# Softmax normalisation of an attention stage: the sums' reciprocal over 128 partitions, by way of DRAM

## The chip, the cores and the metric

One Trainium2 chip, all 8 cores. Each core computes one of the 8 batch rows, with no exchange between cores. The metric is the device time of the slowest core in microseconds.

## The reference

A layer on x of 8 x 2048 x 1024: layer norm, then attention (16 heads of 64, causal, with a linear position bias) and a gated FFN with quantised activations and ternary weights, both added to x. The part that is touched is the softmax division:

```
xn = layernorm(x)
scores = einsum('bhqd,bhkd->bhqk', q, k) / sqrt(64) + alibi_bias   # -inf above the diagonal
attn = softmax(scores, axis=-1)
out = einsum('bhqk,bhkd->bhqd', attn, v)
x = x + out @ w_out + b_out + ffn(xn)
```

## The kernel before

The program is written as one list of instructions; each engine takes its own in that order, and waits are counted semaphores. `B.op` makes every instruction of an engine other than TensorE wait for the one before it on its engine. `B.dma` issues on a named queue: "sync" is SP's, "gpsimd" is POOL's; a `gate` is waited for on that queue first, so everything behind it on the queue waits too.

Phases: layer norm with V projection, attention (from about 440 to 1390 us in the trace), output projection, FFN gate and up, FFN down. Beside the first two phases a generator (`pump`) quantises the three FFN weight matrices: a pass with an Abs on ScalarE (L693) for each of 32 tiles, then a pass with three VectorE operations (L723, L725, L728) and a store by POOL. The tiles are loaded by SP into two buffers.

Attention runs over 8 head pairs (hp). Each begins with the Q and K projection (L446, L450; evicted by ScalarE, L460 and L464). Then come two blocks qh of two 512-column query groups j each. A block walks over key steps (j, ki), ki being a tile of 128 keys. A step issues for both heads (loc 0, 1): the score matmul (L568), the exponential on ScalarE (L581), and on the diagonal memsets and a triangular mask on VectorE (L591, L595). The PV matmul (L501) of step si - 2 follows. V has a column of ones, so row 64 of the output bank is the softmax sum. Score banks rotate over three for each head, `SPOOL`; a bank is free when its reader has finished. Every second step pumps once.

When the last key of a group is done, `_norm_part1` copies the sum row (ScalarE, L522) into `srow`, the 64 output rows into `o_un` (L524), and starts a reciprocal on one partition (VectorE, L527). `part2` broadcasts the reciprocal to 64 partitions by an fp32 matmul with a row of ones (L536) into the first score bank of its head, multiplies (VectorE, L542), and stores to `s_attn` (POOL). `part2` is put into `norm_pending`; a step runs one of them when more than three are pending, in the last block (hp 7, qh 1) when any is. Norms are numbered 0 to 63 in the prediction, in this order; even ones are loc 0, odd ones loc 1.

Of the kernel before, what the change touches and what calls it, by code (L numbers as in the profile page):

```python
# [11 lines left out]
F32 = mybir.dt.float32  # L12
BF16 = mybir.dt.bfloat16
AF = mybir.ActivationFunctionType
ALU = mybir.AluOpType
# [84 lines left out]
class Builder:  # L100
    def __init__(self):
        nc = bass.Bass("TRN2", target_bir_lowering=False)
        self.nc = nc
        self.sched = []
        self.C = defaultdict(int)
        self.stack = contextlib.ExitStack()
        self.sem = {s: self.stack.enter_context(nc.semaphore(s))
                    for s in ("TS", "VS", "SS", "GS", "SY")}

        d = nc.dram_tensor  # L110
        self.x = d("x", [L, D], F32, kind="ExternalInput").ap()
        self.w_in = d("w_in", [D, 3 * D], F32, kind="ExternalInput").ap()
        self.b_in = d("b_in", [3 * D], F32, kind="ExternalInput").ap()
        self.w_out = d("w_out", [D, D], F32, kind="ExternalInput").ap()
        self.b_out = d("b_out", [D], F32, kind="ExternalInput").ap()
        self.w_gate = d("w_gate", [INNER, D], F32, kind="ExternalInput").ap()
        self.w_up = d("w_up", [INNER, D], F32, kind="ExternalInput").ap()
        self.w_down = d("w_down", [D, INNER], F32, kind="ExternalInput").ap()
        self.y = d("y", [L, D], F32, kind="ExternalOutput").ap()
        self.s_xnb = d("s_xnb", [L, D], BF16).ap()  # L120
        self.s_n = d("s_n", [L, D], BF16).ap()
        self.s_attn = d("s_attn", [D, L], BF16).ap()
        self.s_acc = d("s_acc", [L, D], F32).ap()
        self.s_mg = d("s_mg", [INNER, D], BF16).ap()
        self.s_mu = d("s_mu", [INNER, D], BF16).ap()
        self.s_md = d("s_md", [D, INNER], BF16).ap()
        self.s_n2 = d("s_n2", [L, INNER], BF16).ap()

        eb_np, m01_np = _make_consts()
        self.c_eb = nc.inline_tensor(eb_np, name="c_eb")  # L130
        self.c_m01 = nc.inline_tensor(m01_np, name="c_m01")
        self.n_eb = eb_np.shape[1]

        self.fa = Arena(nc, "fa", F32, 8832)
        self.ba = Arena(nc, "ba", BF16, 88320)
# [24 lines left out]
        self.P = [nc.alloc_psum_tensor(f"pb{i}", [128, 512], F32) for i in range(8)]  # L160
        self.bguard = {i: [] for i in range(8)}
# [211 lines left out]
    def ph_attention(self):  # L373
        B = self
        ba, fa = B.ba, B.fa
# [10 lines left out]
        o_un = [ba.alloc(512, parts=65) for _ in range(8)]  # L386
        srow = fa.alloc(2048, parts=1)
        oun_guard = [[] for _ in range(8)]
        B.r_row = fa.alloc(2048, parts=1)
        rr_guard = [[] for _ in range(4)]  # L390
        wstage2 = B.att_wstage
        stg_cons = B.att_stg_cons
        tv = [("TX%d" % p, B.C["TX%d" % p]) for p in range(2)]
# [9 lines left out]
        sa_guard = [[], []]  # L403
        norm_pending = []
        oun_next = [0]

        def emit_norm(maxn=1):
            for _ in range(maxn):
                if not norm_pending:
                    return  # L410
                norm_pending.pop(0)()

        def load_wqk(hp2):
            par2 = hp2 % 2
# [14 lines left out]
        B.waitg("scalar", B.ln_final)  # L429
        B.waitg("vector", B.ln_final)  # L430
        B.ln_final = None
        wq_cast_next = load_wqk(0)
        qk_guard2 = [[], []]
        for hp in range(8):
# [5 lines left out]
            for qk in range(2):  # L440
                for tc in range(4):
# [3 lines left out]
                    for c in range(ND - 1):  # L445
# [3 lines left out]
                            start=(cc == 0), stop=False))  # L449
# [26 lines left out]
            for qh in range(2):  # L476
# [30 lines left out]
                            _norm_part1(loc2, j2, hp, qh, [g])  # L507

                def _norm_part1(loc2, j2, hp2, qh2, vlast):
                    while len(norm_pending) > 3:  # L510
                        emit_norm(1)
                    h2 = 2 * hp2 + loc2
                    jj = j2 % 2
                    obank = OBANK[loc2]
                    Ob = B.P[obank]
                    pu = oun_next[0]
                    oun_next[0] = (pu + 1) % 8
                    B.waitg("scalar", vlast)
                    B.waitg("scalar", oun_guard[pu])
                    ru = pu % 4  # L520
                    B.waitg("scalar", rr_guard[ru])
                    gs0 = B.op("scalar", lambda e, b=Ob, r2=ru: e.copy(  # L522
                        out=srow[0:1, 512 * r2:512 * r2 + 512], in_=b[64:65, :]))
                    gs_ = B.op("scalar", lambda e, b=Ob, p2=pu: e.copy(out=o_un[p2][0:64, :], in_=b[0:64, :]))  # L524
                    B.bguard[obank] = [gs_]
                    B.waitg("vector", [gs0])
                    gr = B.op("vector", lambda e, r2=ru: e.reciprocal(  # L527
                        out=B.r_row[0:1, 512 * r2:512 * r2 + 512],
                        in_=srow[0:1, 512 * r2:512 * r2 + 512]))

                    def part2(loc3=loc2, h3=h2, jj3=jj, qh3=qh2, pu3=pu, ru3=ru, gr3=gr, gs3=gs_):
                        rbank = SPOOL[loc3][0]
                        Rb = B.P[rbank]
                        B.waitg("tensor", [gr3])
                        B.waitg("tensor", B.bguard[rbank])
                        gt = B.op("tensor", lambda e, b=Rb, r2=ru3: e.matmul(  # L536
                            b[0:64, :], B.ones_row64[0:1, :],
                            B.r_row[0:1, 512 * r2:512 * r2 + 512], start=True, stop=True))
                        rr_guard[ru3] = [gt]
                        B.waitg("vector", [gt, gs3])  # L540
                        B.waitg("vector", sa_guard[jj3])
                        gv = B.op("vector", lambda e, b=Rb, p2=pu3, j2=jj3: e.tensor_tensor(  # L542
                            out=o_attn[0:64, 512 * j2:512 * j2 + 512],
                            in0=o_un[p2][0:64, :], in1=b[0:64, :], op=ALU.mult))
                        oun_guard[pu3] = [gv]
                        B.bguard[rbank] = [gv]
                        B.waitg("gpsimd", [gv])
                        sa_guard[jj3] = [B.dma("gpsimd",
                            B.s_attn[64 * h3:64 * h3 + 64, 1024 * qh3 + 512 * jj3:1024 * qh3 + 512 * jj3 + 512],
                            o_attn[0:64, 512 * jj3:512 * jj3 + 512], "SA%d" % jj3)]  # L550
                        B.store_done[h3] = B.store_done[h3] + sa_guard[jj3]
                    norm_pending.append(part2)

                final_blk = (hp == 7 and qh == 1)
                for si, (j, ki) in enumerate(keys):
                    sp = si % 3
                    if len(norm_pending) > (0 if final_blk else 3):
                        emit_norm(1)
                    for loc in locs:
                        st_ = stepmap[loc].get((j, ki))  # L560
                        if st_ is None:
# [46 lines left out]
            wqk_guard[par] = list(qk_guard[-1:])  # L608
            qk_guard2[par] = list(qk_guard[-1:])
            qk_guard = []  # L610
        emit_norm(100)
        B.pump(10 ** 6)
        ba.reset(); fa.reset()
        B.ba.reset()
# [360 lines left out]
```

How the kernel before makes its waits and increments, by code:

```python
    def wait(self, engine, sem, val):  # L171
        if val > 0:
            self.em(engine, lambda e, s=self._sem(sem), v=val: e.wait_ge(s, v))
# [8 lines left out]
    def dma(self, queue, out, in_, sem, transpose=False, slow=False, gate=()):  # L182
        sh = self._sem(sem)
        self.waitg(queue, gate)
        self.C[sem] += 16
        v = self.C[sem]
        if transpose:
            self.em(queue, lambda e, o=out, i=in_, s=sh: e.dma_start_transpose(out=o, in_=i).then_inc(s, 16))
        else:
            self.em(queue, lambda e, o=out, i=in_, s=sh, sl=slow: e.dma_start(out=o, in_=i, allow_slow_non_contiguous=sl).then_inc(s, 16))
        return (sem, v)
# [7 lines left out]
        def run(e, f=fn, sh=self.sem[s], p=prev, vv=v):  # L199
            if p > 0:
                e.wait_ge(sh, p)
            return f(e).then_inc(sh, 1)
```

## Time and profile before

| | us |
|---|---|
| time before, median of 2 runs | 2307.33 |
| the two runs | 2310.09, 2304.57 |
| the profiled execution | 2303.03 |
| its span on the slowest core | 2301.5 |
| spans of the 8 cores | 2279.4 to 2301.5 |

The profile shows one execution on the slowest core, number 6. Times in its rows count from the first instruction. "Idle before" is the time that an engine sat idle ahead of an instruction, and the name behind the arrow is what released it.

### The profile page before, as it was taken

Reading aid. Unit: us, or ns where it says so; the run is one execution under the profiler, and the core shown is the slowest. Engines: PE = TensorE matmul, PEld = TensorE weight load, DVE = VectorE, ACT = ScalarE, POOL = GpSimd, SP = SyncE. Lnnn points to the kernel's source line nnn. Section 1 sums busy time; section 2 is a strip of 40 time slices with the busy share of each in tenths; the row PEclk is TensorE's granted clock in tenths of the full one; section 3 lists DMA queues with packets and bytes.
Section 4 is the critical chain, followed back from the end, with each engine's and each line's share of the span. In section 5 each row is a group of like instructions: output and inputs, shape, how many; then the busy total and the mean of one; then the engine's idle time right before and its main releaser. Section 6 shows DMA issues by size and latency. Waiting matters only on the chain.

```text
span 2301.5 us, 22849 instructions; the slowest of 8 cores (2279.4 to 2301.5 us)
## 1 busy us (share of the span) xinstructions
PE 1429.1 (62%) x5215; PEld 512.3 (22%) x5304; DVE 1009.3 (44%) x1639; ACT 755.7 (33%) x1150; POOL 163.9 (7%) x276
## 2 busy tenths in 40 slices
PE   0004444466756465665647660777999999709997
PEld 0001111111211121111112110223444444304443
DVE  3006667464466764335665430213555555501110
ACT  0762222456644446866445460010122222100000
POOL 2000111100001110000110000000000000000000
PEclk9996666755656565666667575898999999959999
DMA  5774554332334443424543008783000000394661
GB/s 147 245 230 134 182 170 164 122 111 82 112 98 127 146 142 106 140 78 125 161 133 91 18 4 168 230 204 87 37 37 37 37 37 39 75 224 122 153 156 55
DMA packets 277094, 274.27 MB, mean 119 GB/s; under 512 B 208226, under 2 KB 224738, under 8 KB 276964
## 3 DMA queue, kind: packets, MB, share of 16 engines
q1 hardware_dynamic: 256740, 205.68, 33.6%
q0 software_dynamic: 20224, 67.12, 7.7%
q8 instruction: 49, 0.80, 0.1%
q14 instruction: 81, 0.66, 0.1%
HBM read 155.32 MB, written 67.11 MB: 97 GB/s over the span
## 4 chain that ended last, share of the span: by engine, by line
PE 45%; DVE 22%; DMA 12%; ACT 10%; issue 8%; SPq 2%; DVEq 1%; POOL 0%; ACTq 0%; POOLq 0%
PE pb L904 9%; PE pb L824 8%; PE pb L802 8%; DVE fa L527 7%; ACT ba L581 6%; PE pb L446 5%; PE pb L501 4%; PE pb L653 3%; DVE ba L763 3%; PE pb L568 2%; DVE ba L725 2%; DVE ba L723 2%; DMA fa<-w_gate 2%; SPq L188 2%; DMA ba<-s_md 2%
## 5 line engine op out<-in xcount | busy, mean ns | idle before, releaser
L581 ACT ACTIVATE ba<-pb,fa 128x512 bf16<-128x512 f32 (+2 forms) x522 | 339.0, 649 | 266.1 <-PE pb L568 222.2
L501 PE MATMUL pb<-ba 128*65 128x512 bf16 x502 | 230.3, 552 | 184.2 <-DVE ba L595 131.7
L752 PE MATMUL pb<-ba 128*128 128x512 bf16 x251 | 91.8, 528 | 296.3 <-DVE ba L358 169.6
L904 PE MATMUL pb<-ba 128*128 128x512 bf16 x971 | 220.5, 382 | 67.9 <-DMA ba<-s_n 66.9
L527 DVE RECIPROCAL fa<-fa 1x512 f32<-1x512 f32 x64 | 213.8, 3341 | 50.0 <-ACT fa L522 44.7
L568 PE MATMUL pb<-ba 64*128 64x512 bf16 (+2 forms) x502 | 136.7, 516 | 157.5 <-DVE ba L542 156.4
L824 PE MATMUL pb<-ba 128*128 128x512 bf16 x876 | 214.0, 382 | 24.4 <-DMA ba<-s_mu 23.6
L802 PE MATMUL pb<-ba 128*128 128x512 bf16 x875 | 213.1, 381 | 6.6 <-DVE fa L788 5.8
L812 ACT ACTIVATE fa<-pb,fa 128x512 f32<-128x512 f32 x128 | 88.0, 687 | 364.3 <-PE pb L806 364.2
L834 DVE SCALAR_TENSOR_TENSOR fa<-pb,fa 128x512 f32<-128x512 f32 x128 | 96.1, 751 | 157.5 <-PE pb L828 157.2
L904 PEld LDWEIGHTS pb<-ba 128*128 128x128 bf16 x992 | 97.6, 99 | 186.3 <-issue 71.2
L446 PE MATMUL pb<-ba 128*128 128x512 bf16 x433 | 120.6, 421 | 17.6 <-POOL ba L423 14.7
L915 DVE SCALAR_TENSOR_TENSOR fa<-pb,fa 128x512 f32<-128x512 f32 x32 | 24.0, 751 | 244.8 <-PE pb L908 134.9
L536 PE MATMUL pb<-fa 1*64 1x512 f32 x128 | 113.9, 1019 | 21.9 <-DVE fa L527 11.3
L595 DVE TENSOR_TENSOR ba<-ba 128x128 bf16<-128x128 bf16 x256 | 57.7, 226 | 143.3 <-ACT ba L581 94.0
L824 PEld LDWEIGHTS pb<-ba 128*128 128x128 bf16 x896 | 88.2, 98 | 131.3 <-issue 27.1
L802 PEld LDWEIGHTS pb<-ba 128*128 128x128 bf16 x896 | 88.0, 98 | 112.6 <-issue 8.0
L693 ACT ACTIVATE ba<-fa 128x1024 bf16<-128x1024 f32 x96 | 101.5, 1057 | 27.8 <-DMA fa<-w_gate 17.0
L501 PEld LDWEIGHTS pb<-ba 128*65 128x65 bf16 x502 | 44.4, 134 | 296.3 <-issue 296.3
L591 DVE MEMSET ba<- 128x128 bf16 (+2 forms) x247 | 60.6, 245 | 109.1 <-ACT ba L581 45.3
L568 PEld LDWEIGHTS pb<-ba 64*128 64x128 bf16 x502 | 31.8, 98 | 338.8 <-issue 336.2
L752 PEld LDWEIGHTS pb<-ba 128*128 128x128 bf16 x256 | 29.1, 123 | 347.9 <-issue 340.2
(101 smaller groups left out, 1320.5 us busy)
## 6 DMA issues: line engine op xcount, KB each, us to landing
fa<-w_gate SPq DMA_DIRECT2D x64, 512.0 KB, 5.0
fa<-w_up SPq DMA_DIRECT2D x64, 512.0 KB, 3.9
fa<-w_down SPq DMA_DIRECT2D x64, 512.0 KB, 4.1
fa<-x SPq DMA_DIRECT2D x48, 512.0 KB, 5.4
s_n<-ba POOLq DMA_DIRECT2D x32, 512.0 KB, 2.9
fa<-w_in SPq DMA_DIRECT2D x24, 512.0 KB, 6.3
s_mg<-ba POOLq DMA_DIRECT2D x32, 256.0 KB, 5.6
s_mu<-ba POOLq DMA_DIRECT2D x32, 256.0 KB, 4.4
```

What stands on the lines that cost most here:

```text
L446: B.em("tensor", lambda e, b=Pb, cc=c, q=qk, t=tc, p=par: e.matmul(b[:], wqk[p][:, 1024 * q + 128 * cc:1024 * q + 128 * cc + 128], xn_fm[c ...
L501: g = B.op("tensor", lambda e, ob=B.P[obank], k=ki2, hh=h2, pb=pbuf2, f1=first, l1=lastk: e.matmul(ob[0:65, :], v_sb[:, 1040 * k + 65 * hh ...
L527: gr = B.op("vector", lambda e, r2=ru: e.reciprocal(out=B.r_row[0:1, 512 * r2:512 * r2 + 512], in_=srow[0:1, 512 * r2:512 * r2 + 512]))
L536: gt = B.op("tensor", lambda e, b=Rb, r2=ru3: e.matmul(b[0:64, :], B.ones_row64[0:1, :], B.r_row[0:1, 512 * r2:512 * r2 + 512], start=True ...
L568: tg = B.op("tensor", lambda e, b=Sb, l=loc, k=ki, a=wlo, z=whi, kf=k_fm, qf=q_fm: e.matmul(b[0:128, 0:z - a], kf[64 * l:64 * l + 64, 128 ...
L581: eg.append(B.op("scalar", lambda e, b=Sb, q=qg0, g0=gw, a=wlo, c=col, pb=pbuf, jj=j: e.activation(out=pb[:, q - 512 * jj:q - 512 * jj + g ...
L693: gv = B.op("scalar", lambda e, i=idx, c0=col: e.activation(out=sg[0], in_=wb[i], func=AF.Abs, accum_out=accs[:, c0:c0 + 1]))
L752: B.em("tensor", lambda e, b=Pb, cc=c, t=ts_, hh=half: e.matmul(b[:], xn_fm[cc][:, 128 * t:128 * t + 128], wv_sb[:, 1024 * cc + 512 * hh:1 ...
L802: B.em("tensor", lambda e, b=bg_, cc=c, tt=t, o=oc: e.matmul(b[:], n_fm[cc][:, 128 * tt:128 * tt + 128], mg[cc][:, 512 * o:512 * o + 512], ...
L824: B.em("tensor", lambda e, b=bu_, cc=c, tt=t, o=oc: e.matmul(b[:], n_fm[cc][:, 128 * tt:128 * tt + 128], mu[cc][:, 512 * o:512 * o + 512], ...
L834: gh = B.op("vector", lambda e, b=bu_, tt=t, o=oc, hs=h_sb: e.scalar_tensor_tensor(out=hs[:, 512 * o:512 * o + 512], in0=b[:], scalar=B.dq ...
L904: B.em("tensor", lambda e, b=Pb, cc=c, lt=tl, hh=half, nf=n2f: e.matmul(b[:], nf[cc][:, 128 * lt:128 * lt + 128], md[cc][:, 512 * hh:512 * ...
```

## The change

A norm's reciprocal is computed on 128 partitions. POOL writes the sum row to a DRAM scratch `s_d1` and reads it back as 128 x 4. VectorE takes the reciprocal of 128 x 4, splits it into a bf16 high part and a bf16 rest (`rhls`, 128 x 8), with memsets of a scrap tile `vjk` between the steps. SP writes the 128 x 8 to `s_d2` and reads it back as two rows of 512. A matmul with K = 2 and bf16 ones adds the two rows and broadcasts them. The norm is emitted in three deferred pieces with due steps counted from its end (6, 8 and 10), at most two pieces a step; the last block emits all that is pending at every step. More than nine pending pieces force an emission ahead of the next norm.

```
+        self.s_d1 = d("s_d1", [4, 512], F32).ap()
+        self.s_d2 = d("s_d2", [4, 1024], BF16).ap()
...
-        def emit_norm(maxn=1):
-            for _ in range(maxn):
-                if not norm_pending:
+        def emit_norm(maxn=10 ** 6, due=None):
+            n = 0
+            while norm_pending and n < maxn:
+                if due is not None and norm_pending[0][0] > due:
                     return
-                norm_pending.pop(0)()
+                norm_pending.pop(0)[1]()
+                n += 1
...
-                    while len(norm_pending) > 3:
+                    while len(norm_pending) > 9:
                         emit_norm(1)
...
-                    B.waitg("vector", [gs0])
-                    gr = B.op("vector", lambda e, r2=ru: e.reciprocal(
-                        out=B.r_row[0:1, 512 * r2:512 * r2 + 512],
-                        in_=srow[0:1, 512 * r2:512 * r2 + 512]))
+                    B.waitg("gpsimd", [gs0])
+                    d1a = B.dma("gpsimd", B.s_d1[ru], srow[0:1, 512 * ru:512 * ru + 512],
+                                "NB%d" % (ru % 2), gate=g_d1[ru] + last_nb[ru % 2])
+                    g_srow[ru] = [d1a]
+                    d1b = B.dma("gpsimd", s4s[ru], B.s_d1[ru].rearrange("(p c) -> p c", c=4),
+                                "NB%d" % (ru % 2), gate=[d1a] + g_s4[ru])
...
+                    def part2a(ru3=ru, d1g=[d1b]):
+                        B.waitg("vector", d1g)
+                        B.waitg("vector", g_rhlw[ru3])
+                        B.op("vector", lambda e, r3=ru3: e.reciprocal(out=r4b[:], in_=s4s[r3]))
+                        B.op("vector", lambda e: e.memset(vjk[:], 0.0))
+                        B.op("vector", lambda e, r3=ru3: e.tensor_copy(out=rhls[r3][:, 0:4], in_=r4b[:]))
+                        B.op("vector", lambda e: e.memset(vjk[:], 0.0))
+                        B.op("vector", lambda e: e.tensor_copy(out=hif[:], in_=r4b[:]))
+                        B.op("vector", lambda e, r3=ru3: e.tensor_copy(out=hif[:], in_=rhls[r3][:, 0:4]))
+                        B.op("vector", lambda e: e.memset(vjk[:], 0.0))
+                        B.op("vector", lambda e, r3=ru3: e.tensor_tensor(
+                            out=rhls[r3][:, 4:8], in0=r4b[:], in1=hif[:], op=ALU.subtract))
+                        B.op("vector", lambda e: e.memset(vjk[:], 0.0))
+                        gva = B.op("vector", lambda e: e.memset(vjk[:], 0.0))
...
+                    def part2b(ru3=ru):
+                        d2a = B.dma("sync", B.s_d2[ru3].rearrange("(p c) -> p c", c=8), rhls[ru3],
+                                    "NQ%d" % (ru3 % 2), gate=[ev["gva"]] + g_d2[ru3] + last_nq[ru3 % 2])
+                        g_rhlw[ru3] = [d2a]
+                        d2b = B.dma("sync", r2s[ru3].rearrange("t (p c) -> t p c", c=4),
+                                    B.s_d2[ru3].rearrange("(p t2 c) -> t2 p c", t2=2, c=4),
+                                    "NQ%d" % (ru3 % 2), gate=[d2a] + g_r2[ru3])
...
+                    def part2c(loc3=loc2, h3=h2, jj3=jj, qh3=qh2, pu3=pu, ru3=ru, gs3=gs_):
...
-                        B.waitg("tensor", [gr3])
+                        B.waitg("tensor", [ev["d2b"]])
                         B.waitg("tensor", B.bguard[rbank])
-                        gt = B.op("tensor", lambda e, b=Rb, r2=ru3: e.matmul(
-                            b[0:64, :], B.ones_row64[0:1, :],
-                            B.r_row[0:1, 512 * r2:512 * r2 + 512], start=True, stop=True))
-                        rr_guard[ru3] = [gt]
+                        gt = B.op("tensor", lambda e, b=Rb, r3=ru3: e.matmul(
+                            b[0:64, :], ones2[:], r2s[r3], start=True, stop=True))
+                        g_r2[ru3] = [gt]
...
-                    norm_pending.append(part2)
+                    norm_pending.append((st0 + 6, part2a))
+                    norm_pending.append((st0 + 8, part2b))
+                    norm_pending.append((st0 + 10, part2c))
...
-                    if len(norm_pending) > (0 if final_blk else 3):
-                        emit_norm(1)
+                    B.gstep += 1
+                    if final_blk:
+                        emit_norm(10 ** 6)
+                    else:
+                        emit_norm(2, due=B.gstep)
```

## Rows read from the trace of the kernel before

**Rows 1.** Sum over eight stretches of attention, and the page's clock in 40 slices.
```profile
sum 927.00, PE 560.88 PEld 142.86 DVE 503.32 ACT 511.26 POOL 82.52; mean PE 70.11 PEld 17.86 DVE 62.91 ACT 63.91 POOL 10.32
...
PEclk9996666755656565666667575898999999959999
```

**Rows 2.** Waits in attention: who waited for whom, us, times, longest.
```profile
ACT ba L581 <- PE pb L568: 221.1, 60, 12.6
...
ACT fa L522 <- PE pb L536: 18.0, 21, 1.0
...
PE pb L568 <- DVE ba L542: 156.4, 33, 11.4
```

**Rows 3.** Timeline of one pair's end: start, us, engine, line, operation, idle before.
```profile
1302.47 3.67 PE L536 MATMUL pb<-fa 1*64 1x512 f32 x4
...
1303.12 3.34 DVE L527 RECIPROCAL fa<-fa 1x512 f32<-1x512 f32 x1 [1.76 <-ACT fa L522]
...
1310.79 0.68 DVE L542 TENSOR_TENSOR ba<-ba,pb 64x512 bf16<-64x512 bf16 x1
...
1311.62 0.80 PE L568 MATMUL pb<-ba 64*128 64x512 bf16 x2 [5.48 <-DVE ba L542]
...
1312.41 1.47 ACT L581 ACTIVATE ba<-pb,fa 128x512 bf16<-128x512 f32 x2 [6.58 <-PE pb L568]
```

**Rows 4.** The page's groups: reciprocal and fp32 broadcast, busy us, mean ns, idle.
```profile
L527 DVE RECIPROCAL fa<-fa 1x512 f32<-1x512 f32 x64 | 213.8, 3341 | 50.0 <-ACT fa L522 44.7
...
L536 PE MATMUL pb<-fa 1*64 1x512 f32 x128 | 113.9, 1019 | 21.9 <-DVE fa L527 11.3
```

**Rows 5.** Timeline: steady stretches of ScalarE, and a pair of bf16 matmuls.
```profile
915.90 3.03 ACT L581 ACTIVATE ba<-pb,fa 128x512 bf16<-128x512 f32 x4
...
920.27 3.03 ACT L581 ACTIVATE ba<-pb,fa 128x512 bf16<-128x512 f32 x4
...
1325.32 15.52 ACT L581 ACTIVATE ba<-pb,fa 128x512 bf16<-128x512 f32 x20 [0.85 <-PE pb L568]
...
1301.51 1.03 PE L501 MATMUL pb<-ba 128*65 128x512 bf16 x2 [1.26 <-DVE ba L595]
```

**Rows 6.** Small VectorE operations: two of the timeline, one group of the lines.
```profile
6.93 0.06 DVE L236 MEMSET fa<- 128x1 f32 x1 [6.93 <-DMA fa<-b_out]
7.12 0.06 DVE L237 MEMSET fa<- 128x1 f32 x1
...
L351 DVE TENSOR_SCALAR fa<-fa 128x1 f32<-128x1 f32 x16 | 2.5, 154 | 1.7
```

**Rows 7.** DMA issues: two of the timeline, two of the page (KB each, us to landing).
```profile
1.93 2.96 SPq L190 DMA_DIRECT2D fa<-b_in  x3
4.95 0.23 SPq L190 DMA_DIRECT2D fa<-b_out  x1
...
fa<-w_down SPq DMA_DIRECT2D x64, 512.0 KB, 4.1
...
s_attn<-ba POOLq DMA_DIRECT2D x64, 64.0 KB, 2.0
```

**Rows 8.** ScalarE's timeline: three waits of other kinds.
```profile
669.13 10.05 ACT L581 ACTIVATE ba<-pb,fa 128x512 bf16<-128x512 f32 x13 [10.17 <-PE pb L568]
...
868.78 1.47 ACT L581 ACTIVATE ba<-pb,fa 128x512 bf16<-128x512 f32 x2 [2.13 <-PE pb L568]
...
1271.37 9.27 ACT L581 ACTIVATE ba<-pb,fa 128x512 bf16<-128x512 f32 x12 [3.32 <-PE pb L568]
```

**Rows 9.** The last block: timeline of ScalarE, and the chain's last store.
```profile
1340.92 0.58 ACT L522 COPY fa<-pb 1x512 f32<-1x512 f32 x1
...
1354.98 18.63 ACT L581 ACTIVATE ba<-pb,fa 128x512 bf16<-128x512 f32 x24 [0.85 <-PE pb L568]
...
1375.85 0.58 ACT L522 COPY fa<-pb 1x512 f32<-1x512 f32 x1 [2.23 <-PE pb L501]
...
1388.18 2.70 DMA s_attn<-ba
```

More of the change, by code:

```diff
@@ L388, in ph_attention @@
         oun_guard = [[] for _ in range(8)]
-        B.r_row = fa.alloc(2048, parts=1)
-        rr_guard = [[] for _ in range(4)]
+        s4_all = fa.alloc(16)
+        s4s = [s4_all[:, 4 * k:4 * k + 4] for k in range(4)]
+        r4b = fa.alloc(4)
+        hif = fa.alloc(4)
+        vjk = fa.alloc(4)
+        rhl_all = ba.alloc(32)
+        rhls = [rhl_all[:, 8 * k:8 * k + 8] for k in range(4)]
+        r2blk = fa.alloc(1024, parts=2).bitcast(BF16)
+        r2s = [r2blk[0:2, 512 * k:512 * k + 512] for k in range(4)]
+        ones2 = fa.alloc(32, parts=2).bitcast(BF16)
+        g_srow = [[] for _ in range(4)]
+        g_s4 = [[] for _ in range(4)]
+        g_rhlw = [[] for _ in range(4)]
+        g_d1 = [[] for _ in range(4)]
+        g_d2 = [[] for _ in range(4)]
+        g_r2 = [[] for _ in range(4)]
+        last_nb = {0: [], 1: []}
+        last_nq = {0: [], 1: []}
         wstage2 = B.att_wstage
@@ L405, in ph_attention @@
         oun_next = [0]
-        def emit_norm(maxn=1):
-            for _ in range(maxn):
-                if not norm_pending:
+        B.gstep = 0
+        def emit_norm(maxn=10 ** 6, due=None):
+            n = 0
+            while norm_pending and n < maxn:
+                if due is not None and norm_pending[0][0] > due:
                     return
-                norm_pending.pop(0)()
+                norm_pending.pop(0)[1]()
+                n += 1
         def load_wqk(hp2):
@@ L431, in ph_attention @@
         B.ln_final = None
+        g12 = B.op("vector", lambda e: e.memset(ones2[:], 1.0))
+        B.op("vector", lambda e: e.memset(vjk[:], 0.0))
+        B.waitg("tensor", [g12])
         wq_cast_next = load_wqk(0)
@@ L520, in _norm_part1 @@
                     ru = pu % 4
-                    B.waitg("scalar", rr_guard[ru])
+                    B.waitg("scalar", g_srow[ru])
                     gs0 = B.op("scalar", lambda e, b=Ob, r2=ru: e.copy(
@@ new lines, in _norm_part1 @@
+                    g_srow[ru] = [d1a]
+                    d1b = B.dma("gpsimd", s4s[ru], B.s_d1[ru].rearrange("(p c) -> p c", c=4),
+                                "NB%d" % (ru % 2), gate=[d1a] + g_s4[ru])
+                    g_d1[ru] = [d1b]
+                    last_nb[ru % 2] = [d1b]
+                    st0 = B.gstep
+                    ev = {}
+                    def part2a(ru3=ru, d1g=[d1b]):
[10 more added lines that the diff above has]
+                            out=rhls[r3][:, 4:8], in0=r4b[:], in1=hif[:], op=ALU.subtract))
+                        B.op("vector", lambda e: e.memset(vjk[:], 0.0))
+                        gva = B.op("vector", lambda e: e.memset(vjk[:], 0.0))
+                        g_s4[ru3] = [gva]
+                        ev["gva"] = gva
@@ new lines, in part2b @@
+                    def part2b(ru3=ru):
[5 more added lines that the diff above has]
+                                    "NQ%d" % (ru3 % 2), gate=[d2a] + g_r2[ru3])
+                        g_d2[ru3] = [d2b]
+                        last_nq[ru3 % 2] = [d2b]
+                        ev["d2b"] = d2b
@@ L610, in ph_attention @@
             qk_guard = []
-        emit_norm(100)
+        emit_norm(10 ** 6)
         B.pump(10 ** 6)
```

1 line of the change is left out of this document (removed).

## Prediction

> **What bounds the kernel now.** I read the stretches by engine first. The change lies inside attention, from 463 to 1390 us. There no engine is full: in these 927 us TensorE is busy 561, ScalarE 511 and VectorE 503, and the granted clock stands at 5 to 7 tenths, so it is mostly at the lower level, 1.2 GHz [rows 1]. What counts is therefore who waits, and the waits say it: the score exponentials (L581) wait 221.1 us for score matmuls, and these in turn wait 156.4 us for the normalising multiply L542 [rows 2].
>
> One such wait, read from the timeline, shows the reader the pattern [rows 3]. Two heads end a block together. VectorE runs reciprocal, multiply, reciprocal, multiply, and only then (1311.62) may the next score matmul write its bank, since each multiply reads a broadcast that sits in a score bank. ScalarE idles 6.58 us before 1312.41. The reciprocal on one partition costs 3.34 us, 213.8 us over 64 norms; the broadcast as fp32 costs 113.9 us of TensorE, 1.78 a norm [rows 4]. There are 32 such pairs of norms. At the end of a head pair one broadcast falls behind the Q/K projection and costs little, so about three of the four pairs of each head pair give the full wait.
>
> Between the waits ScalarE is the pace: four exponentials (two key steps) start every 4.37 us where a weight tile's Abs (L693) runs on ScalarE, and 1.55 us a step where it doesn't, 20 in 15.52 [rows 5].
>
> **The change, part by part.**
> Removed: 64 long reciprocals and 64 fp32 broadcasts. The new broadcast has K = 2 in bf16; a pair of 512-column bf16 matmuls takes 1.03 us at the low clock [rows 5], so I take 0.5 instead of 1.78. At the end of each head pair a broadcast stands right ahead of the projection, which TensorE alone sets; 7 times about 1.4 us saved there, -10.
>
> Added on VectorE: ten dependent small operations per norm. Five memsets at a pitch of 0.20 us, and five others at 154 ns plus 0.1 us between (1.7 us idle for 16) give 1.0 + 1.3 = 2.3 us [rows 6]. VectorE is thus relieved by only 3.34 + 0.1 - 2.3 = 1.1 us a norm.
>
> Added on POOL's queue: write 2 KB, read it back as 128 x 4. POOL is held until the write has landed, about 2.0 us as the 64 KB store of s_attn [rows 7], plus 0.5 of issue, so some 6 us for two norms. Behind it wait the weight stores and the s_attn stores; weight buffers are two deep, which is 4 steps, 6.2 to 8.7 us. I count this as hidden. The data are wanted 6 key steps later, so the first round trip (about 5 us) is hidden too, outside the last block.
>
> Added on SP's queue: write 128 x 8 bf16, wait, read back as 2 x 128 runs of 8 bytes. The write: 2.1 us as the s_attn store [rows 7]. For the read no row has this shape. Below, b_out, one row on one partition: issued 4.95, VectorE released 6.93, 2.0 us. Above, the b_in loads, two of the three made of 4-byte runs: issued from 1.93, all landed before 6.93, 5.0 us [rows 6, 7]. I take the middle, 3.5 us, since 256 runs lie between one and two thousand. Behind SP wait the weight loads, which land 4.1 us after issue [rows 7] and are issued about 4 steps ahead: nearly hidden, I add 8 us over the stage.
>
> By the Trainium skill, "DMA: Bandwidth & Descriptors", section "Why a DMA increments its semaphore by 16 and not by 1", a transfer is spread over the largest number of engines up to 16 that divides the slowest dimension of both sides. That dimension is 2 for the read back, so two engines would carry 128 runs each; no row here shows such a transfer, and by this rule the upper half of the bracket is the likelier.
>
> **Where the new wait falls.** I counted the emission from the plans. Every norm queues three pieces: (a) the small operations, due 6 steps on, (b) the SP transfers, due 8, (c) broadcast and multiply, due 10. The queue is first in, first out, and two norms enter at the same step. So the first goes at +6, +8, +10, but the second's (a) goes only at +10, behind the first's (c), and its (b) and (c) go together at +11. TensorE meets the wait for a transfer that SP has just been given. This holds for the odd norms 1 to 55, that is 28 times (seven of them through the forced emission above nine pending). Nothing else can run on TensorE, since its queue is in order.
>
> Length of it, from the start of the first broadcast: matmul 0.5, multiply 0.7 and hand-overs 0.2, small operations 2.3, write 2.1, read 3.5, hand-overs 0.3: 9.6 us. The next score matmul ends 1.1 us later, 10.7. TensorE got there 1.1 us after an exponential ended, so ScalarE sees 11.8 us against stored work of three steps: 4.5 us without Abs, about 6.4 with it. It idles 7.3 or 5.4, mean near 6.4. 28 x 6.4 = 179. In the first three head pairs norms come every 3 to 7 steps and the first broadcast waits as well, 12 x 1 = 12. Together 191 us.
>
> What it replaces: 221.1 us of waits of L581, less 22.4 after 1290.8 (last block, below), and 18.0 of L522 for the fp32 broadcasts [rows 2]: 216.7. Not all goes: seven starts of a head pair keep some 1.3 of 3.3 us, the weight pass that ends at 669 and its like keep 12, and short waits of 2.1 us on masks, six of them, 13 [rows 8]. So 216.7 - 9 - 12 - 13 = 183. Net of the regular part: 191 - 183 - 10 + 8 = +6 us.
>
> **The last block** (hp 7, qh 1) empties the list at once. At its first step eleven pieces go out, (b) of norm 56 to (c) of norm 59. First round trip done at 1302.5 + 5.6 + 0.5 + 0.7 = about 1309.6, then three cycles of 9.6: 1338.4, ahead of any score matmul. Before, scores resume at 1311.62 [rows 3], but four old broadcasts slow the next steps until 1325.32 [rows 5]; after, four steps from 1338.4 + 0.9 end at 1345.6. +20. In the middle pair both chains stand in front of the next step, with POOL's trip now uncovered: sums 1341.6 + 4.4 + 2.3 + 5.6 + 1.3 = 1355.2, + 9.6 = 1364.8, two steps to 1368; before 1354.98 [rows 9]. +13. At the end, from 1376.4 the same [rows 9]: 4.4 + 2.3 + 5.6 + 1.3 + 9.6 + store 3.2 = 1402.8, before 1388.18 + 2.70 = 1390.9. +12. Together +45.
>
> **Sum.** 6 + 45 = +51 on the profiled execution of 2303.0 us: 2354. The median shown is 4.3 us above it, so I forecast 2358, +2.2%. Nothing outside attention changes.
>
> **Rivals.** (1) The transfer back is quick, 2.1 us: each of 28 waits is 1.4 shorter, -39, the last block's eight cycles -11: 2308, no change. For it: 2.0 us landings of small transfers; against: 8-byte runs. Chance 0.27. (2) The read takes 5 us, or both transfers queue behind a 512 KB load in SP's ring, 1.5 to 3 more each time: 36 x 1.5 to 3 = +54 to +108: 2412 to 2466. For it: SP's loads are in flight much of the time; against: while SP is held for the second norm it issues none. Chance 0.25. The rule above, with two engines at the price of the upper row, gives the first of these, 2412. (3) Faster: TensorE's wait is covered, for instance because ScalarE holds more stored work or because the old waits freed were larger than I took. Its place is the step +11, its price 6.4 us each; it decides from 28 x 6.4 down to 28 x 2.9, so that the last block's 45 is paid and 46 gained: the chain would have to be 9.6 - 3.5 = 6.1 us or less, of which the parts on TensorE and VectorE and the hand-overs take 4.0 and leave 2.1 for two transfers of 2.0 each. Then about 2250. Chance 0.10. That the reciprocals don't leave the chain is excluded by the code. The forecast itself, 2335 to 2390: 0.38.
>
> **Numbers.** Range 2300 to 2440: it leaves out faster (0.10) and the far end of rival 2 (0.10). A change under 2% can't be told from none here, that is 2261 to 2353. Faster 0.10, within 0.40 (rival 1 and the lower third of the forecast), slower 0.50.
>
> **What would show it.** Right: VectorE's reciprocals gone and its attention share down by about 70 us; the new broadcast with idle of 5 to 8 us before them, released by a transfer into the two-row tile, some 30 times; attention longer by about 50 us, most of it after the start of the last block. Wrong: landings of the SP pair far from 2.1 and 3.5 us; weight loads or stores that reach ScalarE or VectorE late; TensorE's clock falling or rising in attention, which I take as unchanged.

## The result and the profile after

The changed kernel takes 2507.4 us (median of 11 runs) where the kernel before takes 2308.3 (10 runs): ratio 1.0845, 95% interval 1.0819 to 1.0871, so 8.5% slower. The forecast was 2358, at most 2440. Below, a time in us worked out from a ratio is the ratio times 2308; the changed kernel is then 2503. Some runs of either kernel fall into a slower state of the chip, and the ratios leave them out.

All of it lies in attention. The first matmul of the output projection, same core (0), before and after (the lists of one line: duration min/median/max, first to last start):

```profile
L653 PE MATMUL pb<-ba x250: 378/379/634, 1440.6 to 1511.0; 128*128 128x512 bf16 x125
```

```profile
L715 PE MATMUL pb<-ba x250: 378/379/631, 1653.5 to 1723.2; 128*128 128x512 bf16 x125
```

It starts 213 us later; the first projection matmul of attention starts at 416 and 421. Attention with the transposes behind it is thus 208 us longer on this core, and 201 and 196 on cores 2 and 6, against 195 by the ratio.

Waits of the changed kernel (who waited for whom: us, times, longest). L594 is the new broadcast, L599 its multiply, L630 the score matmul, L643 the exponential, L785 and L755 the weight quantisation on VectorE and ScalarE, `s_d` either DRAM scratch:

```profile
ACT ba L643 <- PE pb L630: 371.4, 86, 27.9
...
PE pb L594 <- DMA fa<-s_d: 320.9, 48, 14.0
...
PE pb L630 <- DVE ba L599: 95.7, 28, 10.1
...
DVE ba L785 <- DMA fa<-w_down: 47.2, 12, 8.7
...
ACT ba L755 <- DMA fa<-w_up: 37.8, 10, 7.2
```

The wait that the change was to remove did go down, score matmuls behind the multiply from 156.4 [rows 2] to 95.7 us. But TensorE now waits 320.9 us for the read back from DRAM, and ScalarE 371.4 instead of 221.1. The groups of the reciprocal and the broadcast, which answer to [rows 4]:

```profile
L564 DVE RECIPROCAL fa<-fa 128x4 f32<-128x4 f32 x64 | 11.4, 178 | 37.8 <-DMA fa<-s_d 31.3 <-DVE ba L599 0.5 <-DVE ba L657 0.2
...
L594 PE MATMUL pb<-fa 2*64 2x512 bf16 x64 | 37.5, 586 | 328.8 <-DMA fa<-s_d 320.9 <-ACT ba L643 3.6 <-ACT ba L548 2.4
```

Both did what they should: 213.8 us of reciprocals became 11.4, 113.9 of broadcasts 37.5.

A pair of norms as the forecast described it, in the timeline (start, us, engine, line, operation, idle before):

```profile
1055.61 0.63 PE L594 MATMUL pb<-fa 2*64 2x512 bf16 x1
...
1056.56 0.68 DVE L599 TENSOR_TENSOR ba<-ba,pb 64x512 bf16<-64x512 bf16 x1 [7.58 <-PE pb L594]
...
1057.34 0.18 DVE L564 RECIPROCAL fa<-fa 128x4 f32<-128x4 f32 x1
...
1059.73 0.33 SPq L192 DMA_DIRECT2D s_d<-ba  x1
...
1061.63 0.26 SPq L192 DMA_DIRECT2D fa<-s_d  x1
...
1064.86 0.60 PE L594 MATMUL pb<-fa 2*64 2x512 bf16 x1 [7.08 <-DMA fa<-s_d]
...
1066.20 0.69 ACT L643 ACTIVATE ba<-pb,fa 128x512 bf16<-128x512 f32 x1 [4.08 <-PE pb L630]
```

First broadcast, multiply, small operations, write, read back, second broadcast: 9.25 us where 9.6 were forecast.

Other pairs are worse, and this the forecast did not have. The chain of waits between 1193 and 1224:

```profile
1193.82 4.69 DMA fa<-s_d
...
1201.12 4.32 DMA s_d<-ba
...
1205.92 6.06 DMA fa<-w_down
...
1212.21 0.77 DVE ba L785
...
1214.73 0.69 DVE ba L599
...
1217.89 2.87 DMA s_d<-ba
...
1220.88 2.59 DMA fa<-s_d
...
1223.74 0.61 PE pb L594
```

The first row is POOL's read of an even norm's sums. SP's write of that norm lands after 4.32 us; only then do the read back and, behind it, the weight load go out (1205.92). VectorE waits for that tile before it reaches the multiply of the same norm (1214.73), behind which stand the small operations of the odd norm. TensorE's broadcast then comes after 13.54 us of waiting. SP's own waits in attention:

```profile
SPq L175 <- DVE fa L574: 624.0, 60, 41.4
...
SPq L175 <- DMA s_d<-ba: 110.0, 64, 4.3
```

### The profile page after: what moved, and what is told of

The parts are those of the page before. It is cut to its first block, busy times and chain, and to the rows that moved or that the text cites. A ratio compares the mean times of both kernels' runs of the same rounds, so it can differ in the third digit from the quotient of the medians.

```text
span 2524.0 us, 24778 instructions; the slowest of 8 cores (2475.9 to 2524.0 us)
## 1 busy us (share of the span) xinstructions
PE 1402.7 (56%) x5151; PEld 508.7 (20%) x5240; DVE 870.2 (34%) x2217; ACT 755.1 (30%) x1150; POOL 236.2 (9%) x404
## 4 chain that ended last, share of the span: by engine, by line
PE 41%; DMA 23%; DVE 15%; issue 9%; ACT 7%; SPq 2%; DVEq 1%; POOL 0%; ACTq 0%; POOLq 0%
PE pb L966 9%; PE pb L886 8%; PE pb L864 8%; DMA fa<-s_d 5%; PE pb L470 5%; DMA s_d<-ba 4%; ACT ba L643 3%; PE pb L525 3%; DMA fa<-w_gate 3%; PE pb L715 2%; DVE ba L825 2%; DMA fa<-w_up 2%; SPq L190 2%; DVE ba L785 2%; DMA ba<-s_md 2%
## 5 line engine op out<-in xcount | busy, mean ns | idle before, releaser
L643 ACT ACTIVATE ba<-pb,fa 128x512 bf16<-128x512 f32 (+2 forms) x522 | 338.9, 649 | 412.7 <-PE pb L630 371.4
L525 PE MATMUL pb<-ba 128*65 128x512 bf16 x502 | 241.2, 577 | 187.6 <-DVE ba L657 88.5
L814 PE MATMUL pb<-ba 128*128 128x512 bf16 x251 | 92.4, 531 | 298.2 <-DVE ba L360 170.2
L966 PE MATMUL pb<-ba 128*128 128x512 bf16 x971 | 219.9, 382 | 64.0 <-DMA ba<-s_n 63.0
L886 PE MATMUL pb<-ba 128*128 128x512 bf16 x876 | 225.8, 398 | 19.8 <-DMA ba<-s_mu 18.8
L864 PE MATMUL pb<-ba 128*128 128x512 bf16 x875 | 227.3, 400 | 7.1 <-DVE fa L850 5.9
L594 PE MATMUL pb<-fa 2*64 2x512 bf16 x64 | 37.5, 586 | 328.8 <-DMA fa<-s_d 320.9
L630 PE MATMUL pb<-ba 64*128 64x512 bf16 (+2 forms) x502 | 141.8, 525 | 105.1 <-DVE ba L599 95.7
L470 PE MATMUL pb<-ba 128*128 128x512 bf16 x433 | 127.1, 438 | 24.5 <-POOL ba L444 13.8
L966 PEld LDWEIGHTS pb<-ba 128*128 128x128 bf16 x992 | 97.5, 98 | 181.9 <-issue 66.2
L755 ACT ACTIVATE ba<-fa 128x1024 bf16<-128x1024 f32 x96 | 101.4, 1056 | 72.0 <-DMA fa<-w_up 37.8
L886 PEld LDWEIGHTS pb<-ba 128*128 128x128 bf16 x896 | 90.8, 101 | 135.5 <-issue 61.5
L864 PEld LDWEIGHTS pb<-ba 128*128 128x128 bf16 x896 | 91.3, 102 | 123.6 <-issue 52.5
L599 DVE TENSOR_TENSOR ba<-ba,pb 64x512 bf16<-64x512 bf16 x64 | 43.5, 679 | 205.2 <-PE pb L594 191.8
L785 DVE TENSOR_SCALAR ba<-fa 128x1024 bf16<-128x1024 f32 x96 | 72.3, 753 | 90.8 <-DMA fa<-w_down 47.2
L814 PEld LDWEIGHTS pb<-ba 128*128 128x128 bf16 x256 | 29.2, 124 | 350.0 <-issue 342.4
```

The costliest lines, as they stand in the source:

```text
L470: B.em("tensor", lambda e, b=Pb, cc=c, q=qk, t=tc, p=par: e.matmul(b[:], wqk[p][:, 1024 * q + 128 * cc:1024 * q + 128 * cc + 128], xn_fm[c ...
L525: g = B.op("tensor", lambda e, ob=B.P[obank], k=ki2, hh=h2, pb=pbuf2, f1=first, l1=lastk: e.matmul(ob[0:65, :], v_sb[:, 1040 * k + 65 * hh ...
L630: tg = B.op("tensor", lambda e, b=Sb, l=loc, k=ki, a=wlo, z=whi, kf=k_fm, qf=q_fm: e.matmul(b[0:128, 0:z - a], kf[64 * l:64 * l + 64, 128 ...
L643: eg.append(B.op("scalar", lambda e, b=Sb, q=qg0, g0=gw, a=wlo, c=col, pb=pbuf, jj=j: e.activation(out=pb[:, q - 512 * jj:q - 512 * jj + g ...
L755: gv = B.op("scalar", lambda e, i=idx, c0=col: e.activation(out=sg[0], in_=wb[i], func=AF.Abs, accum_out=accs[:, c0:c0 + 1]))
L785: B.op("vector", lambda e, i=idx, w=wname: e.tensor_scalar(out=sg[0], in0=wb[i], scalar1=B.wsv[w], scalar2=0.5, op0=ALU.mult, op1=ALU.is_ge))
```

## The experiments

**1. Sorted pieces.** `norm_pending.sort(key=lambda z: z[0])` after the three appends.

> The changed kernel with one edit: the list of deferred pieces is sorted by due step, so that both norms of a pair do their small operations at +6, their SP transfers at +8 and their broadcasts at +10. Theory A (the first-in-first-out list makes TensorE wait for transfers just issued, and SP's queue, held for the second norm, makes weight loads late): the waits of the new broadcast, 320.9 us in 48 cases, fall to about 140 (last block and a few dense early steps), and the time falls by 28 x 5.5 = 150 us or more, to about 2340. Rival B (the loss is mostly weight loads held behind SP's waits on VectorE, whatever the order of the pieces): the waits move to VectorE and ScalarE waiting for weight tiles, and the time falls by less than 70 us.

Ratio 1.0878 (1.0781 to 1.0975): no faster at all. Yet the broadcast's waits fell as theory A expected (L599 multiply, L631 score matmul):

```profile
PE pb L631 <- DVE ba L599: 219.6, 52, 14.3
...
PE pb L594 <- DMA fa<-s_d: 153.7, 37, 14.7
...
DVE ba L599 <- DMA s_attn<-ba: 125.1, 29, 14.0
```

The broadcast's wait halved, and a new one took its place: both multiplies of a pair write the same slot of `o_attn`, and the second now waits for the first one's store, which POOL issues late. Score matmuls wait behind it, 219.6 us. The waits for weight tiles grew too, from 124 to 174 us.

**2 and 3. SP's transfers on POOL's queue**, in the change's order and sorted.

```
-                        d2a = B.dma("sync", ...
+                        d2a = B.dma("gpsimd", ...
-                        d2b = B.dma("sync", ...
+                        d2b = B.dma("gpsimd", ...
```

> The changed kernel with one edit: the write and the read back of the split reciprocal are issued by POOL and not by SP, so that SP's weight loads are never held. Order of the pieces as in the changed kernel. Theory A: SP's 624 us of waiting for the last small operation go, VectorE's and ScalarE's waits for weight tiles (47 + 33 + 38 + 6 us) fall to about 25 as before, and the time falls by 60 to 110 us, to about 2400 to 2445; the broadcast still waits about 5.5 us in 28 cases. Rival B: falls by more than 120. Rival C (holding SP costs nothing, as the forecast had it but for 8 us): within 15 us of 2507.

> Both edits together: sorted pieces and POOL's transfers. Theory A: neither stall is left but in the last block, 2290 to 2330. Were the two costs one and the same, this would equal the better of the two single edits.

Ratios 1.2188 (1.2095 to 1.2281) and 1.1510 (1.1457 to 1.1563): far slower. With the first edit alone the weight tiles were in time: 25 us of waits, 15.0 of them VectorE's for w_down, where the changed kernel has 124. But POOL now holds four transfers a norm with two landings, in line with the stores, and TensorE waits 736 us for the read back. The issue of a load by POOL, both kinds of read together, is 851 ns, where the changed kernel's is 580:

```profile
L192 POOL DMA_DIRECT2D fa<-s_d x128 | 109.0, 851 | 429.2 <-DMA s_d<-ba 128.7 <-DMA s_d<-fa 102.4 <-issue 67.0
```

This edit changed two things at once, so it says nothing of what SP's holding costs.

**4 and 5. What was removed, measured alone.** In the kernel before, the reciprocal is replaced by nothing (the broadcast reads a constant); then the broadcast is the K = 2 bf16 one as well.

> The kernel before without its 64 reciprocals: the broadcast reads a constant row, and waits for the copy of the sum row as before, so the division is left out. This measures what taking the reciprocals off can be worth at most while the fp32 broadcast stays. The forecast took 183 us of ScalarE's waits as removed by reciprocal and broadcast together. Theory A: at least 150 us faster, near 2150. Rival D (the removed waits were over-counted, which would explain the miss without SP): less than 80 us faster.

> The kernel before without its reciprocals, and with the K = 2 bf16 broadcast of a constant: both costs that the change removes are gone, nothing is added (the division is left out). It measures the term 'what it replaces' as a whole, forecast at 183 + 10 us. Attention was 893 to 920 us without the reciprocals alone, against 1024 to 1033. Theory: another 50 to 65 us, attention near 840 and the time near 2125. Then the changed kernel adds near 380 us of its own where 244 were forecast.

The first takes 2188 us, some 120 below before (two runs, so no interval). The second has ratio 0.9327 (0.9305 to 0.9350), 155 us below. ScalarE then waits 83.5 us for score matmuls, not 221:

```profile
ACT ba L582 <- PE pb L569: 83.5, 45, 7.6
...
PE pb L569 <- DVE ba L543: 59.0, 29, 8.2
```

So leaving both out is worth 155 us, where I had taken 193; and the change adds 350 of its own, where I had 244.

**6. Sorted, and four slots of `o_attn`.**

```
-        o_attn = ba.alloc(1024)
+        o_attn = ba.alloc(2048)
+                    so = 2 * loc2 + jj
```

Slot, guard and semaphore then go by `so` and not by `jj`.

> Sorted pieces as in the first experiment, and the tile o_attn with four slots, one for each head and half, where it had two, so that the second multiply of a pair no longer waits for the first one's store (125.1 us of VectorE's waits there). Theory A2 (sorting took the waits off the broadcast, 320.9 to 153.7 us, and handed them to this slot): VectorE's waits for the s_attn store fall below 10 us and the time falls by 80 us or more, to about 2430. Rival B2 (what bounds is SP and VectorE in order, and the slot's wait only covers it): less than 40 us.

Ratio 1.0420 (1.0366 to 1.0475): 98 us below the changed kernel, and VectorE's waits for the s_attn store are gone. Theory A2 holds: the stall of the order and the slot that covered it are worth 98 us together, and sorting alone nothing. The four slots alone were not tried, but in the changed kernel VectorE's multiplies show no wait for that store, so they had nothing to take off there.

**7 to 10. Weight loads one pump earlier on SP's list; the last block; both placed right.**

```
                     cons_guard[idx] = [gv]
+                    kk += 1
+                    load(kk)
                     yield
...
-                    if final_blk:
-                        emit_norm(10 ** 6)
-                    else:
-                        emit_norm(2, due=B.gstep)
+                    emit_norm(2, due=B.gstep)
```

`load(kk)` puts the next tile's load on SP's list, gated by its own buffer. The four kernels, in this order: earlier loads alone; with sorted pieces and four slots; with the last block by due step too; the same with the early loads in attention only.

> The changed kernel with one edit: each weight tile's load is put on SP's list one pump (two key steps) earlier, ahead of the SP transfers that it used to stand behind; buffers and their guards stay. Theory A3 (SP held by the transfers' waits makes weight loads late, and a VectorE that waits for a weight tile makes the multiplies and small operations behind it late): VectorE's and ScalarE's waits for weight tiles (about 120 us) fall by half or more, the long waits of the broadcast, those over 9 us, go, and the time falls by 60 to 100 us. Rival (late weights only fill time that TensorE's waits leave anyway): less than 25 us.

> The three edits together: sorted pieces, four slots, weight loads earlier. If both theories hold the gains add to 150 us or more: 2330 to 2360, of which the last block's emptied list is still about 45 us.

> The three edits, and the last block emits by due step like the others instead of all that is pending. The forecast priced the emptied list at 45 us, of which the two trips after the last key stay (12): 25 to 35 us below the run with three edits, near or just under the time before.

> As the run with all four edits (sorted pieces, four slots, earlier weight loads, last block by due step), but the earlier weight loads begin only with attention, since in layer norm they stood in front of the x loads and cost 160 us there. Attention itself should stay at 1024 to 1036 us, the same as before the change. Theory: total 2295 to 2325, no gain left from the change even with its stalls taken off.

Ratios 1.1408 (1.1357 to 1.1458), 1.0831 (1.0783 to 1.0879), 1.0722 (1.0653 to 1.0790) and 1.0045 (1.0020 to 1.0070). The first three are spoilt by layer norm, where the x loads now stand behind a weight load whose buffer isn't free yet, so that attention starts at about 580 us and not at 418:

```profile
ACT fa L346 <- DMA fa<-x: 92.1, 5, 18.7
```

Attention alone, from its first projection matmul to the output projection's first (cores 0, 2 and 6), runs 1022 to 1033 us in the kernel before, 1223 to 1233 in the changed one, 1175 to 1199 with earlier weights only, 1108 to 1139 with sorted pieces and slots, 1051 to 1066 with all three, 1024 to 1036 with the last block too. Earlier loads are thus worth some 40 us alone and 60 behind the other two edits, and the emptied list of the last block 25 by the ratios. Theory A3 holds in part: with earlier loads alone the waits for weight tiles fall from 124 to 26 us, but the broadcast's waits of over 9 us stay (12 of them on core 2). With the early loads confined to attention (1026 to 1042 us there) the kernel is about where the kernel before was, 2318: these edits win back what the change had lost, and no more. TensorE still waits 156.8 us for the read back.

**11. Broadcast at +13 instead of +10.**

> The run above with the broadcast due at +13 and not +10. Its TensorE still waits 156 us for the read back in 41 cases, some 35 of them outside the end. Theory E (the distance between transfers and broadcast is too short for a trip that queues behind weight loads): these waits fall by half and the time by 40 to 80 us, below the time before. Rival F (the trip is late by what SP waits for, and moves with it): under 20 us.

Ratio 1.0029 (0.9990 to 1.0068), against 1.0045: no difference. TensorE's wait for the read back falls from 156.8 to 33.2 us, but score matmuls now wait 106.4 us for the multiply, 32.5 before. In experiment 9:

```profile
PE pb L597 <- DMA fa<-s_d: 156.8, 42, 14.3
...
PE pb L631 <- DVE ba L602: 32.5, 34, 5.0
```

and with +13 (core 0 of both kernels shows the same: 160.3 to 37.0 us, and 33.5 to 108.2):

```profile
PE pb L631 <- DVE ba L602: 106.4, 47, 13.1
...
PE pb L597 <- DMA fa<-s_d: 33.2, 9, 12.9
```

Rival F's number came, but not its reason: the wait for the trip does go with distance, as theory E had it, and the wait for VectorE takes its place.

**12 to 14. Each trip taken away.** POOL's trip or SP's is left out of the kernel of experiment 9, and SP's out of the changed kernel.

> The kernel of the run with early loads in attention only (2318 us), less POOL's trip through DRAM: the small operations read a constant 128 x 4 tile and wait for the copy of the sum row (the division is by a constant, so that part is left out). 164 us lie between that kernel and the one with neither reciprocal nor fp32 broadcast (2154). Theory G (POOL, held for two landings a norm, delays the s_attn and weight stores, and VectorE waits for the landing in front of the masks): 40 us or more. Rival H (SP's trip holds most of it): less than 20 us.

> The same kernel, less SP's trip instead: the broadcast reads a constant row and waits for the last small operation. POOL's trip stays. Theory H: 80 us or more, to about 2240 or below, since TensorE's 157 us of waits for the read back, late weight tiles and SP's 157 us of waits for its own writes go. Theory G: less than 40 us.

> The changed kernel itself (order of pieces, slots and last block as in the change), less SP's trip. If the order's price is the trip that TensorE stands for at +11, it goes with the trip: 28 x 5.6 + 8 x 5.6 = 200 us off 2507, and the coupling with the weight loads another 50: near 2260. If it stays above 2400, the price lies in the order of VectorE and the s_attn slot and not in SP's transfers.

Ratios 1.0003 (0.9974 to 1.0032), 0.9793 (0.9767 to 0.9819) and 0.9941 (0.9921 to 0.9961). In these three kernels the division is by a constant. POOL's trip is worth 10 us in the mended kernel, and the two intervals overlap, so it can't be told from nothing; theory G is out. SP's is worth 58 us where the order is mended, between the two theories' numbers, and 209 in the change's own order, where 250 were expected. The order in its turn costs 185 us with SP's trip (1.0845 against 1.0045) and 34 without (0.9941 against 0.9793): each is much cheaper without the other. But with no SP trip at all the changed kernel is still 141 us above the one with nothing added. Its waits (L623 score matmul, L592 multiply, L587 broadcast, L575 last small operation):

```profile
ACT ba L636 <- PE pb L623: 197.8, 89, 15.5
...
PE pb L623 <- DVE ba L592: 94.0, 33, 13.8
PE pb L587 <- DVE fa L575: 85.2, 20, 9.1
```

In the mended kernel without SP's trip score matmuls wait for the multiply too,

```profile
PE pb L624 <- DVE ba L595: 105.5, 53, 12.8
```

where with nothing added it was 59.0 (above).

**15 and 16. Ten small operations cut to three**, in the kernel of experiment 9 and in the changed one:

```
+                        B.op("vector", lambda e, r3=ru3: e.tensor_copy(out=rhls[r3][:, 0:4], in_=r4b[:]))
+                        gva = B.op("vector", lambda e, r3=ru3: e.tensor_tensor(
+                            out=rhls[r3][:, 4:8], in0=r4b[:], in1=rhls[r3][:, 0:4], op=ALU.subtract))
```

> The kernel with sorted pieces, four slots, earlier loads in attention and no emptied list (2318 us), and the small operations cut from ten to three: reciprocal, bf16 copy, and the rest as fp32 minus bf16 in one subtraction, without the memsets between. Nothing is left out of the result. Per norm that takes 2.6 - 0.8 = 1.8 us off VectorE, 115 us in all. Theory J (what is left between 2256, without SP's trip, and 2154 is mostly VectorE's time in its own order, as the 214 us of reciprocals were worth 116): half to nine tenths of it shows, 2215 to 2260, faster than both kernels. Rival K (the small operations lie in idle time of VectorE): under 20 us, same as before.

> The changed kernel with only this edit, ten small operations cut to three. The chain that TensorE stands for at +11 is 1.8 us shorter in 28 + 8 cases, 65 us, and VectorE has 115 us less. Theory J: 60 to 110 us faster than the changed kernel, 2400 to 2445. Rival K: 65 us by the chain alone or less.

Ratios 0.9936 (0.9906 to 0.9967) and 1.0531 (1.0503 to 1.0560). In the changed kernel that is 72 us. In the trace the ten operations hold VectorE for 2.4 us and the three for 0.8, so the shorter chain explains some 58 (36 x 1.6) and not 65; what is left over is about the noise, and J and K can't be told apart here. In the mended one it is 25 us: more than nothing, far from the 58 that theory J wanted at least. With it the mended kernel is the first complete one below the kernel before, by 0.6%, which is less than the 2% that would count as a change.

**17. The old reciprocal, only placed apart.** In the kernel before, the reciprocal is a piece due at +2 (odd norms +4), broadcast and multiply one due at +6 (+8).

> The kernel before with its own reciprocal and fp32 broadcast, no transfer, but cut in two deferred pieces: the reciprocal 2 steps (odd norm 4) after the end, broadcast and multiply 6 (odd 8) steps after, so that no multiply that a score matmul waits for stands behind a reciprocal, in the last block too. VectorE's work is unchanged. Theory: most of the 116 us that the reciprocals cost came from where they stood and not from VectorE's time; 50 to 100 us faster than before, 2210 to 2260. Rival: they delay masks and quantisation instead, less than 20 us.

Ratio 1.0053 (1.0031 to 1.0076): the rival's number holds. On core 0 only six multiplies, three of them in the last block, still stand directly behind a pair of reciprocals, and nothing is won; ScalarE still waits 214.4 us for score matmuls, and score matmuls 80.0 for the multiply (core 2: 213.2 and 76.1, where it has 216.5 and 156.4 in the kernel before). What takes the place of the 80 us was not followed.

```profile
ACT ba L591 <- PE pb L578: 214.4, 99, 8.6
...
PE pb L578 <- DVE ba L550: 80.0, 24, 8.7
```

**18. The reciprocal as exp(-log) on ScalarE.**

```
+                    B.op("scalar", lambda e, b=Ob, r2=ru: e.activation(
+                        out=srow[0:1, 512 * r2:512 * r2 + 512], in_=b[64:65, :], func=AF.Ln, scale=9.094947017729282e-13))
...
+                    gr = B.op("scalar", lambda e, r2=ru: e.activation(
...
+                        in_=srow[0:1, 512 * r2:512 * r2 + 512], func=AF.Exp, scale=-1.0, bias=lnb[0:1, 0:1]))
```

The scale is 2^-40, and `lnb` holds -27.7259, which takes it out again.

> The kernel before with the reciprocal on ScalarE: the copy of the sum row becomes a logarithm, and an exponential of its negative (a 1 x 512 operation of about 0.58 us more on ScalarE) replaces VectorE's 3.34 us. No transfer, no other order. Theory: the reciprocals leave the wait as in the run without them (116 us), less 64 x 0.7 = 45 us of ScalarE, which sets the pace in steady stretches: 2210 to 2260, if logarithm and exponential don't make the engine reload its tables; with reloads each norm costs some us more and it is slower than before.

Ratio 0.9528 (0.9507 to 0.9549), 109 us faster, with one more operation of 721 ns a norm on ScalarE and a single table load in attention. The time is all it tells: the result is off by a relative 0.15, for a reason that was not looked into, so as it stands this is no replacement. It shows that taking 3.34 us off VectorE is worth having even at 0.72 on the engine that sets the pace.

## Why the prediction was wrong

**The stalls of the order: right.** The second norm's pieces go together at +11, and TensorE stands through the trip. The chain shown is 9.25 us (9.6 forecast), with 1.9 for the write (2.1) and 3.2 for the read back (3.5); over the 35 read backs in the chain of waits it is 2.3 to 4.6, median 3.1. The rule of the Trainium skill, "DMA: Bandwidth & Descriptors", section "Why a DMA increments its semaphore by 16 and not by 1", made the upper half of the bracket, 3.5 to 5.0, the likelier; 28 of the 35 lie below 3.5, though whether two engines carried the transfer no run here shows. SP's trip was forecast, in its order, at 36 x 5.6 + 8 = 210 us, and measured at 209. That close a match is partly luck: late weight tiles (40 to 60 us) are in the measured number, and stand in mine at 8, and some of the 36 cases overlap with other waits.

**The last block: near, but high.** In its emptied list broadcasts follow at 9.0 us, where I had cycles of 9.6 (the terms of my first sum there give 1309.3 and not 1309.6, which changes nothing):

```profile
1467.79 0.60 PE L594 MATMUL pb<-fa 2*64 2x512 bf16 x1 [1.86 <-ACT fa L546]
1476.80 0.60 PE L594 MATMUL pb<-fa 2*64 2x512 bf16 x1 [8.41 <-DMA fa<-s_d]
1485.82 0.60 PE L594 MATMUL pb<-fa 2*64 2x512 bf16 x1 [8.42 <-DMA fa<-s_d]
```

Emission by due step won 25 us, of the 33 that I had put on the first and middle place.

**The step that failed: the rest of what is added.** Without SP's trip the changed kernel lies 141 us above the kernel with nothing added; my sum has about 34 there (244 less 210). I priced the ten small operations only inside the chain that TensorE stands for, counted the rest of VectorE as relieved by 1.1 us a norm, took POOL's trip as hidden outside the last block, and had no term for what stands ahead of a multiply in VectorE's list. But [rows 3] show that VectorE works in order and that score matmuls wait for multiplies; whatever stands ahead of a multiply or of a small operation, a wait for POOL's landing, a weight tile, quantisation, holds up a broadcast and its score bank.

The kernel without SP's trip shows it (rows of experiment 14 above): ScalarE waits 197.8 us for score matmuls, 114 more than with nothing added, and TensorE waits 85.2 us for the last small operation, about half of that in the last block. One place outside it, on core 5: the even norm's small operations wait 0.68 us for POOL's landing and end at 1203.9; then VectorE works through weight tiles, with a wait of 2.08 us for POOL's store, and reaches that norm's multiply only at 1211.13; the odd norm's small operations end at 1214.2, and its broadcast starts at 1214.42 after a wait of 8.13 us, with no transfer of SP in it.

How much of the 107 us each item bears stays open. VectorE's time alone is not the measure: 214 us of reciprocals were worth 120 in the kernel before, but the 102 us that experiment 15 took off the small operations (64 x 1.6) only 25.

**"What it replaces": 193 forecast, 155 measured.** I added up ScalarE's waits and called the sum removable. A wait ends when the last of several causes ends; without reciprocal and fp32 broadcast 83.5 us of it are still there, where I had left 34 outside the last block. With the shortfall above, 38 + 107 us, this is the miss of 144, within its rounding: forecast +51, measured +195.

**"Weight loads nearly hidden, +8": wrong.** Worth 40 to 60 us. SP is held 624 us for the last small operation, and I followed that only up to the load's issue, not back through VectorE's wait for the tile to the next multiply.

**The rivals.** Rival 1 (read back in 2.1 us) had neither the duration, median 3.1, nor the time. Rival 2's upper part, 2466, came nearest in time, and landings as late as it asked for do occur (4.3 for a write, 4.6 for a read back), but the median read back is 3.1 and not 5. SP's transfers and the weight loads were in each other's way, but by SP's waiting: once issued, a w_down tile lands after 5.0 us, for 4.1 before. TensorE's granted clock between the first and the last broadcast, which I took as unchanged, was 0.60 on core 0 for 0.64 before, and 0.61 for 0.63 on core 6; what that is worth was not separated. Behind attention, the FFN's gate and up matmuls on core 0 took 399 ns for 382, some 30 us, but on core 6 of the same execution 381, so that is not the change's.

**Open.** Of the 107 us between the mended kernel without SP's trip (0.9793) and nothing added (0.9327), POOL's trip is about 10 and seven of ten small operations 25, if those savings add. The rest, some 70, is argued to be VectorE's order (rows of experiments 13 and 5 above: 105.5 against 59.0) and not shown.

## What to carry to other kernels

A deferred list that is first in, first out loses its distances as soon as two items enter together: look at the due step of each piece after the one ahead of it has gone. The price of a round trip through DRAM depends on where it stands: SP's was worth 209 us in one order and 58 in another. On a queue that also feeds another pipeline, follow what it holds through that pipeline back to your own path. On an engine that works in order, look at what stands ahead of each operation that another engine waits for. And before pricing what a change adds, measure what it can win by leaving the operation out: here 155 us, less than the forecast's own stalls (191 + 45).

## What the runs showed of the hardware

In the changed kernel a write of 2 KB from 128 partitions by SP was seen to land in 1.4 to 4.3 us, its read back into two partitions in 2.3 to 4.6, median 3.1. The same two transfers issued by POOL, in line with its others, made the kernel 12% slower than issued by SP. The same 512 reciprocals take 3.34 us as 1 x 512 on VectorE and 0.178 us as 128 x 4. By the Trainium skill, "ScalarE: Activation LUTs", section "Table sets: the hidden batching unit", logarithm and exponential share one set of tables; experiment 18 agrees, with one load of 1.3 us in attention.
